# A state-space layer: decay rows broadcast over the partitions by DMA and masked by GpSimd, the exponential written to PSUM and multiplied from there

## The chip, the cores and the metric

The kernel runs on one core of a Trainium2 chip. The metric is the device time of one execution in microseconds. The kernel before has a median of 2572.7 us over three runs, between 2570.35 and 2581.11.

## What is computed

Two transformer-like layers on 1024 tokens (4 sequences of 256) of 512 features: attention and a sparse feed-forward part, then a state-space layer and a feed-forward part. The change is in the state-space layer alone. It has 128 heads of 64 channels in 8 groups; B and C (128 states) are shared by the 16 heads of a group. Cut to what matters here:

```python
dt = clip(softplus(dt + dt_bias), 0.001, 100)
cs = cumsum(dt * A, axis=time)                 # per head; A = -1 .. -128
Lmat = where(l >= s, exp(cs[l] - cs[s]), 0)    # per head and sequence, 256 x 256
y[l] = sum_s (C[l] . B[s]) * Lmat[l, s] * dt[s] * x[s]
y = y + D * x
out = rmsnorm_per_group(y * silu(gate)) * norm_w @ out_proj.T
```

(The reference scans in chunks of 128; the kernel takes a whole sequence of 256 at once, which is the same sum.)

## The kernel before

**Tiling.** A group g is worked in 8 units j. A unit is 2 heads = 128 channels on the partitions, with 1024 tokens along the columns, in two halves of 512. For each unit TensorE projects four halves (`in_half`: X_0, X_1, G_0, G_1, that is x and the gate), each 12 matmuls of 128x512, since weights and input are split in a high and a low part and multiplied three times. ScalarE takes the last convolution tap from PSUM (`tap`), VectorE the three others (`conv_tap`), ScalarE a tanh, VectorE makes SiLU of it (`silu`).

**The scan.** It goes sequence by sequence, b = 0 to 3. For one (j, b) and one head, s lies on the partitions and l along the columns. Since l >= s, of the 256 x 256 matrix only 384 columns are worked: s in the first block against l of both blocks (256 columns), s in the second block against l of the second (128 columns). The parts:

- `rows` (PE): a matmul with a one-hot column broadcasts the head's row of -cs over the 128 partitions, into PSUM bank 5. The row comes from `comb`, where it lies as three bfloat16 parts that add up to it.
- `clamp` (ScalarE): Relu(row + cs[s]), with cs[s] as bias per partition, from PSUM into the buffer `decay`. For l < s the clamp gives 0.
- `exps` (ScalarE): Exp(-...) over both heads at once, 768 columns, in place.
- `decay` (VectorE): times the scores `b_scores`, into `decayed`. The scores are C.B times a mask of 0.25 and 0, made once a group (`scores`).
- `scan` (PE): `decayed` against `xdt` (x times dt, transposed by `turn` on PE and scaled by `times_dt` on VectorE).
- `skip` (VectorE) adds D*x, `gate` (GpSimd) multiplies by SiLU of the gate, `square` (ScalarE) and `add_square` (GpSimd) gather the squares for the norm. `sq` is one buffer of 512 columns.

**Order.** There is no scheduler: each engine runs its own written sequence (`steps`), and semaphores join them. In step j TensorE projects unit j+1 while it scans unit j. `decay` and `decayed` have two buffers each, by b % 2. GpSimd also makes the low parts of the weights (`weights_lo`), for which SP's next load (`load_in`) waits, three buffers in a ring. Between two groups stand `unit0` (the last step's convolution work) and `project` (norm and output projection). Groups 0 to 6 are a loop, group 7 is written out behind it. ScalarE's order in step j, for j >= 1:

```
exps(j,1)  tap X0  weights_hi  square(j-1,0)  exps(j,2)  tanh X0  tap X1  exps(j,3)
square(j-1,1)  tanh X1  tanh G0  weights_hi  exps(j+1,0)  tanh G1
```

VectorE's:

```
decay(j,0)  conv X0 tap 1  decay(j,1)  skip(j-1,1)  conv X0 taps 2, 3  decay(j,2)  conv X1 tap 1  silu X0
conv X1 taps 2, 3  skip(j,0)  silu X1  silu G0  decay(j,3)  silu G1  times_dt twice
```

Lines: L964 clamp, L970 exponential, L1242 `decay`, L1461 `rows`, L1473 and L1474 `scan`, L1451 to L1453 `in_half`, L1206 convolution, L1226 and L1232 SiLU, L938 `tap`, L954 tanh, L1131 `weights_lo`, L1144 `gate`, L1152 `add_square`.

## Time and profile before

| | |
|---|---|
| median of three runs | 2572.7 us (2570.35 to 2581.11) |
| span of the profiled execution | 2581.9 us; no other time of it is at hand |
| PE / VectorE / ScalarE / GpSimd busy | 2390.2 / 1761.2 / 1368.2 / 802.0 us |
| `rows`, TensorE (L1461) | 512 matmuls |
| clamp and exponential, ScalarE (L964, L970) | 344.2 and 216.7 us |
| `decay`, VectorE (L1242) | 256, 397.9 us, 1554 ns on average |

Busy is the time in which an engine works on at least one instruction; sums over lines can be longer, since neighbours overlap. A chain of waits over the whole program says little here, because the engines are nearly balanced in this layer: what counts is the order within one unit, and so the timeline of one unit is shown below.

### The profile page before, as it was taken

What the parts mean: (1) busy time and instruction counts of PE and PEld (TensorE: products, weight loads), DVE (VectorE), ACT (ScalarE), POOL (GpSimd) and SP (SyncE); (2) the same over time, 40 slices, a digit from 0 to 9 for tenths busy, and PEclk for the clock granted to TensorE, in tenths of its full rate; (3) what the DMA queues carried; (4) which work ended last, traced back from release to release, by engine and by line L of the source; (5) the groups of instructions that cost most, each with busy time, mean ns of one, the idle gap of its engine ahead of it and who ended that gap; (6) DMA issues with size and microseconds to landing.
All of it is one profiled execution on the core that took longest, in us unless ns stands there. A gap on an engine that the chain in (4) does not pass through costs nothing. (4 is left out here: it accounts for less than half of the span.)

```text
span 2581.9 us, 39470 instructions
## 1 busy us (share of the span) xinstructions
PE 2390.2 (93%) x11656; PEld 1672.8 (65%) x11656; DVE 1761.2 (68%) x3109; ACT 1368.2 (53%) x3069; POOL 802.0 (31%) x645
## 2 busy tenths in 40 slices
PE   7989989899799989999989999998999999987998
PEld 4445454454567767767677676776766767756877
DVE  4656566464689579759848957966984985975345
ACT  5325152250488468548638737845854874873230
POOL 3214041130134325414414423432441441441220
PEclk8998989899899999999999999999999999998999
DMA  5000000000211011011011010101101101101100
GB/s 196 1 1 0 0 1 0 1 1 0 94 30 34 23 46 34 19 50 34 27 43 34 27 47 27 33 14 55 34 23 46 34 27 45 34 1 74 49 17 33
DMA packets 36024, 82.95 MB, mean 32 GB/s; under 512 B 3664, under 2 KB 3792, under 8 KB 35168
## 3 DMA queue, kind: packets, MB, share of 16 engines
q1 hardware_dynamic: 35808, 80.38, 9.5%
q8 instruction: 98, 1.61, 0.3%
q14 instruction: 118, 0.97, 0.1%
HBM read 77.48 MB, written 2.88 MB: 31 GB/s over the span
## 5 line engine op out<-in xcount | busy, mean ns | idle before, releaser
L1451 PE MATMUL b_ps<-xh_keep,wh 128*128 128x512 f32 x1152 | 495.3, 430 | 23.1 <-issue 20.1
L1453 PE MATMUL b_ps<-xh_keep,wl 128*128 128x512 f32 x1152 | 468.0, 406 | 0.0
L1452 PE MATMUL b_ps<-xl_keep,wh 128*128 128x512 f32 x1152 | 467.7, 406 | 0.0
L1242 DVE TENSOR_TENSOR decayed<-decay,b_scores 128x768 f32<-128x768 f32 x256 | 397.9, 1554 | 25.7 <-ACT decay L970 24.8
L1131 POOL TENSOR_TENSOR wl<-wraw,wh 128x512 fp32r<-128x512 f32 x144 | 190.6, 1324 | 606.9 <-ACT wh L919 606.9
L1206 DVE SCALAR_TENSOR_TENSOR xs<-b_ps,par,xs 128x510 f32<-128x510 f32 (+2 forms) x384 | 284.7, 742 | 119.9 <-ACT xs L938 107.0
L964 ACT ACTIVATE decay<-b_ps,cs 128x256 f32<-128x256 f32 (+1 forms) x1024 | 344.2, 423 | 7.9 <-PE b_ps L1461 7.7
L1451 PEld LDWEIGHTS b_ps<-xh_keep,wh 128*128 128x128 f32 x1152 | 224.6, 195 | 103.6 <-issue 59.8
L1453 PEld LDWEIGHTS b_ps<-xh_keep,wl 128*128 128x128 f32 x1152 | 224.2, 195 | 54.3
L1452 PEld LDWEIGHTS b_ps<-xl_keep,wh 128*128 128x128 f32 x1152 | 225.6, 196 | 43.1
L1332 DVE SCALAR_TENSOR_TENSOR yl<-yg,par,yh 128x512 fp32r<-128x512 f32 x128 | 96.4, 758 | 201.9 <-ACT yh L985 200.8
L970 ACT ACTIVATE decay<-decay 128x768 f32<-128x768 f32 x256 | 216.7, 846 | 8.1
L1552 PE MATMUL b_ps<-oh,yh 128*128 128x512 f32 x512 | 202.0, 395 | 12.8 <-DVE yl L1332 12.2
L1144 POOL TENSOR_TENSOR yg<-yt,yg 128x512 f32<-128x512 f32 x112 | 180.8, 1615 | 100.6 <-DVE yt L1261 100.5
L985 ACT ACTIVATE yh<-yg,par 128x512 fp32r<-128x512 f32 x128 | 91.7, 722 | 211.4 <-PE b_ps L1554 211.4
L1553 PE MATMUL b_ps<-oh,yl 128*128 128x512 f32 x512 | 200.2, 391 | 0.0
L1554 PE MATMUL b_ps<-ol,yh 128*128 128x512 f32 x512 | 200.0, 391 | 0.0
L1473 PE MATMUL b_ps<-decayed,xdt 128*64 128x256 f32 x1024 | 174.4, 416 | 21.3 <-DVE decayed L1242 21.2
L1152 POOL TENSOR_TENSOR ssq<-ssq,sq 128x512 f32<-128x512 f32 x112 | 144.9, 1293 | 152.8 <-ACT sq L978 152.8
L938 ACT ACTIVATE xs<-b_ps,par 128x512 f32<-128x512 f32 x128 | 98.4, 769 | 137.8 <-PE b_ps L1453 137.8
L296 POOL TENSOR_SCALAR pr<-pr,su 128x256 f32<-128x256 f32 x128 | 118.1, 923 | 108.6 <-DVE su L435 108.6
L1136 POOL TENSOR_TENSOR ol<-oraw,oh 128x512 fp32r<-128x512 f32 x64 | 85.6, 1337 | 210.6 <-ACT oh L926 210.6
(225 smaller groups left out, 4258.2 us busy)
## 6 DMA issues: line engine op xcount, KB each, us to landing
wraw<-win_dram SPq DMA_DIRECT2D x144, 256.0 KB, 2.6
oraw<-wout_dram SPq DMA_DIRECT2D x8, 2048.0 KB, 9.7
w<-w_dram SPq DMA_DIRECT2D x2, 3584.0 KB, 23.7
fraw<-wgu_dram SPq DMA_DIRECT2D x11, 512.0 KB, 3.3
draw<-wd_dram SPq DMA_DIRECT2D x1, 2816.0 KB, 11.2
out_dram<-x_keep SPq DMA_DIRECT2D x8, 256.0 KB, 2.0
wqkv<-wqkv_dram SPq DMA_DIRECT2D x1, 1536.0 KB, 9.1
x_keep<-x_dram SPq DMA_DIRECT2D x1, 1536.0 KB, 30.7
```

Of the source, the lines that this page charges most:

```text
L964: last = nc.scalar.activation(dst, src, ACT.Relu, bias=bias)
L970: nc.scalar.activation(ex[:, b % 2, :, :], ex[:, b % 2, :, :], ACT.Exp, scale=-1.0).then_inc(*exp_done.inc())
L1131: nc.gpsimd.tensor_tensor(wl[:, n % RING, :], wraw[:, n % RING, :], wh[:, n % RING, :].bitcast(F32), ALU.subtract).then_inc(w_lo.sem, 1)
L1144: nc.gpsimd.tensor_tensor(yg[:, j, cols], yt[:, h, :], sg, ALU.mult).then_inc(*gated.inc())
L1206: ins = nc.vector.scalar_tensor_tensor(y[:, :, back:], z[:, :, 0:SEQ - back], param(g, sub, TAPS - 1 - back), y[:, :, back:], ALU.mult, AL ...
L1242: nc.vector.tensor_tensor(sd[:, b % 2, :, :], ex[:, b % 2, :, :], sm[:, b, :].unsqueeze(1).to_broadcast([P, 2, 3 * P]), ALU.mult)\
L1451: nc.tensor.matmul(out, w_h, x_h, start=(k == 0), stop=False)
L1452: nc.tensor.matmul(out, w_h, x_l, start=False, stop=False)
L1453: last = nc.tensor.matmul(out, w_l, x_h, start=False, stop=(k == KT - 1))
L1552: nc.tensor.matmul(ps[t][:], y_h, oh[:, j % 2, :], start=(j == 0), stop=False)
L1553: nc.tensor.matmul(ps[t][:], y_l, oh[:, j % 2, :], start=False, stop=False)
L1554: last = nc.tensor.matmul(ps[t][:], y_h, ol[:, j % 2, :], start=False, stop=(j == UNITS - 1))
```

## The change

The broadcast over partitions goes from TensorE to the DMA queues: the rows of -cs (float32, stored once in DRAM) are read per unit with a partition broadcast into `rows`, two buffers of two heads, four sequences and three blocks of 128 columns, of which the DMA fills the first two. GpSimd (`mask_rows`) adds a constant (0 or a large negative number, `later`) to the two diagonal blocks, one of them into the third place. ScalarE then takes Exp(row - cs[s]) straight from there, without a clamp, and writes it to PSUM, bank 4 for head 0 and bank 5 for head 1. VectorE multiplies from PSUM, one product a head, each with its own semaphore count. The three-way split of the sums in the prologue goes. Banks of other jobs move to make room, and the scores are copied by ScalarE (times 0.25) where VectorE masked them before.

```diff
-        ("pick", (p[:, None] % 32 == np.arange(16)[None, :])),
+        ("later", np.where(p[None, :] >= p[:, None], 0.0, -BIG)),
...
-        ex = sb("decay", [P, 2, 2, 3 * P])
+        rows = sb("rows", [P, 2, 2, BATCH, 3, P])
         sd = sb("decayed", [P, 2, 2, 3 * P])
...
+        EXP_BANK = 4
...
-                for b in range(BATCH):
-                    out.append((f"R{j}_{b}", 5))
-                    out += nxt[b:b + 1]
+                out += nxt
                 if j < UNITS - 1:
-                    out += [(f"Y{j}_0", 6), (f"T{j + 1}_0", 4), (f"T{j + 1}_1", 6), (f"Y{j}_1", 7)]
+                    out += [(f"Y{j}_0", 6), (f"T{j + 1}_0", 6), (f"T{j + 1}_1", 1), (f"Y{j}_1", 7)]
...
-        head_jobs = [(f"CB{b}", 4 + b) for b in range(BATCH)] + [("T0_0", 4), ("T0_1", 6)]
+        head_jobs = [("CB0", 6), ("CB1", 7), ("CB2", 2), ("CB3", 3), ("T0_0", 6), ("T0_1", 7)]
...
+        def decay_of(g, j, b, h):
+
+            at = rows[:, j % 2, h, b]
+            c0, c1 = (ncs[:, ds(g * HPG + ((b * TPB + t) * NH + 2 * j + h), 1)] for t in range(TPB))
+            e = ps[EXP_BANK + h]
+            yield e[:, 0:2 * P].rearrange("p (k c) -> p k c", c=P), at[:, 0:2, :], c0
+            yield e[:, 2 * P:3 * P], at[:, 2, :], c1
...
+            def load_rows(g, j):
+
+                src = ssm["cs_dram"][ds(g * HPG + 2 * j, 2), :].rearrange("h (b c) -> h b c", b=BATCH)
+                for h in range(2):
+                    sp.dma_start(rows[:, j % 2, h, :, 0:2, :].rearrange("p b k c -> p b (k c)"),
+                                 src[h].partition_broadcast(P)).then_inc(rows_loaded[j % 2], 16)
...
+                sp.wait_ge(*exp_done.made(ph, heads[0], back=1))
+                load_rows(i, 1)
                 for n in range(AHEAD, AHEAD + SUBS):
                     load_in(i, n)
                     if n == AHEAD:
                         load_out(i)
-                sp.wait_ge(*bk.filled(ph, f"R{UNITS - 1}_{BATCH - 1}"))
-                load_comb(i + 1)
-            for n in range(AHEAD, SUBS):
-                load_in(LOOPS, n)
-                if n == AHEAD:
-                    load_out(LOOPS)
+                    j = (n - AHEAD) // 2 - 1
+                    if n % 2 == 0 and 0 <= j < UNITS - 1:
+                        sp.wait_ge(*exp_done.made(ph, (j, BATCH - 1, 1)))
+                        load_rows(i, j + 2)
...
-            def clamp(ph, g, j, b):
-
-                name = f"R{j}_{b}"
-                if b >= 2 or j:
-
-                    act.wait_ge(*decayed.made(ph, f"{j}_{b - 2}" if b >= 2 else f"{j - 1}_{b + 2}"))
-                waited(bk.filled(ph, name))
-                for src, dst, bias in blocks(ph, g, j, b):
-                    last = nc.scalar.activation(dst, src, ACT.Relu, bias=bias)
-                last.then_inc(*bk.free(ph, name))
-
             def exps(ph, g, j, b):
-                clamp(ph, g, j, b)
-                act.wait_ge(*bk.drained(ph, f"R{j}_{b}"))
-                nc.scalar.activation(ex[:, b % 2, :, :], ex[:, b % 2, :, :], ACT.Exp, scale=-1.0).then_inc(*exp_done.inc())
+
+                act.wait_ge(*rows_masked.made(g, j))
+                for h in range(2):
+                    if j or b:
+                        waited(decayed.made(ph, (j, b - 1, h) if b else (j - 1, BATCH - 1, h)))
+                    else:
+                        act.sem_inc(act_passed)
+                    for dst, src, bias in decay_of(g, j, b, h):
+                        last = nc.scalar.activation(dst, src, ACT.Exp, bias=bias)
+                    last.then_inc(*exp_done.inc())
+
+            def scores(ph):
+
+                for b in range(BATCH):
+                    name = f"CB{b}"
+                    act.wait_ge(*bk.filled(ph, name))
+                    nc.scalar.activation(sm[:, b, :], ps[bk.bank(ph, name)][:, 0:3 * P], ACT.Copy, scale=0.25)\
+                        .then_inc(*bk.free(ph, name))
...
+            def mask_rows(g, j):
+
+                pool.wait_ge(rows_loaded[j % 2], g * (32 * UNITS // 2) + 32 * (j // 2 + 1))
+                later = cst("later").unsqueeze(1).to_broadcast([P, 2 * BATCH, P])
+                at = rows[:, j % 2].rearrange("p h b k c -> p (h b) k c")
+                nc.gpsimd.tensor_tensor(at[:, :, 2, :], at[:, :, 1, :], later, ALU.add)
+                nc.gpsimd.tensor_tensor(at[:, :, 0, :], at[:, :, 0, :], later, ALU.add).then_inc(rows_masked.sem, 1)
...
+                    if j < UNITS - 1:
+                        mask_rows(g, j + 1)
+                    if j:
                         add_square(ph, j - 1)
...
                 steps(ph, i, False)
+                mask_rows(i, UNITS)
                 add_square(ph, UNITS - 1)
...
-                dve.wait_ge(*exp_done.made(ph, f"{j}_{b}"))
-                nc.vector.tensor_tensor(sd[:, b % 2, :, :], ex[:, b % 2, :, :],
-                                        sm[:, b, :].unsqueeze(1).to_broadcast([P, 2, 3 * P]), ALU.mult)\
-                    .then_inc(*decayed.inc())
+                for h in range(2):
+                    dve.wait_ge(*exp_done.made(ph, (j, b, h)))
+                    nc.vector.tensor_tensor(sd[:, b % 2, h, :], ps[EXP_BANK + h][:, 0:3 * P], sm[:, b, :], ALU.mult)\
+                        .then_inc(*decayed.inc())
...
-            def rows(ph, j, b):
-
-                name = f"R{j}_{b}"
-                pe.wait_ge(*bk.freed(ph, name))
-                for h in range(2):
-                    last = nc.tensor.matmul(ps[bk.bank(ph, name)][:, h * SEQ:(h + 1) * SEQ], sel[:, 2 * j + h:2 * j + h + 1].to_broadcast([32 * SPLITS, P]),
-                                            comb[:, b * SEQ:(b + 1) * SEQ], start=True, stop=True)
-                last.then_inc(*bk.full(ph, name))
...
-                    if j:
-                        rows(ph, j, 1)
                     for b in range(BATCH):
-                        if names and (j or b != 1):
+                        if names:
                             in_half(ph, g, 4 + 2 * j + b // 2, names[b])
-                        if b == 0:
-                            if j:
-                                scan(ph, j - 1, BATCH - 1)
-                            else:
-                                rows(ph, 0, 0)
-                                in_half(ph, g, 4, names[1])
-                                rows(ph, 0, 1)
-                        if b + 2 < BATCH:
-                            rows(ph, j, b + 2)
-                        elif b + 2 == BATCH and not final:
-                            rows(ph, j + 1, 0)
                         if b == 0 and j:
+                            scan(ph, j - 1, BATCH - 1)
                             pe.wait_ge(*bk.drained(ph, f"T{j}_1"))
                         if b + 1 < BATCH:
                             scan(ph, j, b)
```

The other hunks follow from these: `scores` on ScalarE, `ncs` for `cs` with the sign turned, the prologue without `sum_part` and `remainder`, and the same SP loop written out for the last group.

What stands in the queues, shown at three places. On ScalarE at the end of a step, `exps(j+1, 0)` and the tanh of G1 behind it. Before:

```order
L964 ISA [waits b_decayed,b_full5]
L964 ACTIVATE decay<-b_ps5,cs 128x256
L964 ISA
L964 ACTIVATE decay<-b_ps5,cs 128x128
L964 ISA
L964 ACTIVATE decay<-b_ps5,cs 128x256
L964 ISA
L964 ACTIVATE decay<-b_ps5,cs 128x128
L969 REGISTER_ALU
L970 ACTIVATE decay<-decay 128x768 [waits b_free5]
L947 REGISTER_ALU
L954 ACTIVATE tx<-b_ps3 128x512 [waits b_full3,silued]
```

And with the change:

```order
L926 REGISTER_ALU [waits rows_masked]
L977 ISA [waits b_decayed]
L977 ACTIVATE b_ps4<-rows,ncs 128x256
L977 ISA
L977 ACTIVATE b_ps4<-rows,ncs 128x128
L926 REGISTER_ALU
L977 ISA [waits b_decayed]
L977 ACTIVATE b_ps5<-rows,ncs 128x256
L977 ISA
L977 ACTIVATE b_ps5<-rows,ncs 128x128
L959 REGISTER_ALU
L966 ACTIVATE tx<-b_ps3 128x512 [waits b_full3,silued]
```

Four clamps and one exponential in place become four exponentials; the one wait at the head (the product two b earlier, and the filled bank) becomes a wait for each head on `b_decayed`, which is now the product of the b just before.

On GpSimd in the middle of a step, from `gate` (L1144, now L1159) to the first `add_square` (L1152, now L1167). Before:

```order
L1144 TENSOR_TENSOR yg<-yt,yg 128x512 [waits b_free7]
L1149 REGISTER_ALU
L1151 ISA [waits squared]
L1152 TENSOR_TENSOR ssq<-ssq,sq 128x512 [waits sq_added]
L1149 REGISTER_ALU
L1151 REGISTER_ALU [waits squared]
L1152 TENSOR_TENSOR ssq<-ssq,sq 128x512 [waits sq_added]
```

And with the change:

```order
L1159 TENSOR_TENSOR yg<-yt,yg 128x512 [waits b_free7]
L1143 REGISTER_ALU
L1146 TENSOR_TENSOR rows<-rows,consts 128x8x128 [waits rows_loaded0]
L1147 TENSOR_TENSOR rows<-rows,consts 128x8x128
L1164 REGISTER_ALU
L1166 ISA [waits squared]
L1167 TENSOR_TENSOR ssq<-ssq,sq 128x512 [waits sq_added]
L1164 REGISTER_ALU
L1166 REGISTER_ALU [waits squared]
L1167 TENSOR_TENSOR ssq<-ssq,sq 128x512 [waits sq_added]
```

The two additions on the rows of the next unit stand between `gate` and `add_square`.

On TensorE, the end of a projected half, and the scan behind it. Before:

```order
L1453 MATMUL b_ps2<-xh_keep,wl 128x512
L1459 REGISTER_ALU
L1461 MATMUL b_ps5<-comb,sel 128x256 [waits b_free5]
L1461 MATMUL b_ps5<-comb,sel 128x256
L1468 REGISTER_ALU
L1469 REGISTER_ALU [waits b_free7]
L1473 MATMUL b_ps7<-decayed,xdt 64x256 [waits b_decayed]
```

And with the change:

```order
L1459 MATMUL b_ps2<-xh_keep,wl 128x512
L1465 REGISTER_ALU
L1466 REGISTER_ALU [waits b_free7]
L1470 MATMUL b_ps7<-decayed,xdt 64x256 [waits b_decayed]
L1471 MATMUL b_ps7<-decayed,xdt 64x128
```

The two broadcast matmuls with their wait on bank 5 are gone, and the scan follows the projection. In step 0 of a group the second projection stood before scan(0, 0), and now stands behind it.

## Rows read from the trace of the kernel before

**Rows 1.** The page's list of DMA queues: packets, MB, share of 16 engines.

```profile
q1 hardware_dynamic: 35808, 80.38, 9.5%
```

**Rows 2.** Windows, one unit: length, busy us by engine, clock granted, DMA share, GB/s.

```profile
974.93:991.86 16.93, 16.93 (x100) 12.20 (x98) 15.71 (x19) 14.12 (x31) 8.38 (x6) 1.00 0.13 32
```

**Rows 3.** Timeline of PE: start, length, instruction, in an inner unit.

```profile
945.61 0.40 PE L1461 MATMUL b_ps<-comb,sel 96*128 96x256 bf16 x2
945.94 0.66 PE L1473 MATMUL b_ps<-decayed,xdt 128*64 128x256 f32 x4
...
946.74 0.50 PE L1451 MATMUL b_ps<-xh_keep,wh 128*128 128x512 f32 x1
```

**Rows 4.** Timeline of VectorE (DVE), one unit.

```profile
970.23 1.94 DVE L1242 TENSOR_TENSOR decayed<-decay,b_scores 128x768 f32<-128x768 f32 x1
972.64 0.69 DVE L1232 SCALAR_TENSOR_TENSOR yg<-tx,b_ps 128x512 f32<-128x512 f32 x1 [0.46 <-ACT tx L954]
973.24 1.28 DVE L1251 TENSOR_TENSOR xdt<-b_ps,dth 128x512 f32<-128x512 f32 x2
974.44 0.95 DVE L1242 TENSOR_TENSOR decayed<-decay,b_scores 128x768 f32<-128x768 f32 x1
975.86 0.75 DVE L1206 SCALAR_TENSOR_TENSOR xs<-b_ps,par,xs 128x510 f32<-128x510 f32 x1 [0.47 <-ACT xs L938]
976.53 1.89 DVE L1242 TENSOR_TENSOR decayed<-decay,b_scores 128x768 f32<-128x768 f32 x1
978.34 0.73 DVE L1261 SCALAR_TENSOR_TENSOR yt<-xs,par,b_ps 128x512 f32<-128x512 f32 x1
979.00 1.62 DVE L1206 SCALAR_TENSOR_TENSOR xs<-b_ps,par,xs 128x508 f32<-128x508 f32 x2
980.54 1.95 DVE L1242 TENSOR_TENSOR decayed<-decay,b_scores 128x768 f32<-128x768 f32 x1
...
983.07 0.68 DVE L1226 SCALAR_TENSOR_TENSOR xs<-tx,xs 128x512 f32<-128x512 f32 x1
983.67 1.52 DVE L1206 SCALAR_TENSOR_TENSOR xs<-b_ps,par,xs 128x508 f32<-128x508 f32 x2
...
987.15 1.95 DVE L1242 TENSOR_TENSOR decayed<-decay,b_scores 128x768 f32<-128x768 f32 x1
```

**Rows 5.** Timeline of ScalarE (ACT), the same unit.

```profile
968.36 0.63 ACT L954 ACTIVATE tx<-xs 128x512 f32<-128x512 f32 x1 [0.69 <-DVE xs L1206]
968.90 0.58 ACT L954 ACTIVATE tx<-b_ps 128x512 f32<-128x512 f32 x1
...
969.90 1.34 ACT L964 ACTIVATE decay<-b_ps,cs 128x256 f32<-128x256 f32 x4
...
972.02 0.58 ACT L954 ACTIVATE tx<-b_ps 128x512 f32<-128x512 f32 x1
...
974.93 0.78 ACT L938 ACTIVATE xs<-b_ps,par 128x512 f32<-128x512 f32 x1 [0.21 <-PE b_ps L1453]
```

**Rows 6.** Timeline of GpSimd (POOL), the same unit.

```profile
976.30 1.30 POOL L1131 TENSOR_TENSOR wl<-wraw,wh 128x512 fp32r<-128x512 f32 x1 [2.98 <-ACT wh L919]
...
980.38 1.29 POOL L1152 TENSOR_TENSOR ssq<-ssq,sq 128x512 f32<-128x512 f32 x1
```

**Rows 7.** Groups of instructions by line, shapes apart: count, busy us, mean ns.

```profile
L1268 DVE TENSOR_TENSOR b_scores<-b_ps,scan_mask 128x384 f32<-128x384 f32 x32 | 15.5, 546 | 0.0
...
L1792 POOL TENSOR_TENSOR fl<-fraw,fh 128x1024 fp32r<-128x1024 f32 x11 | 26.3, 2392 | 98.3 <-ACT fh L1747 98.3
```

**Rows 8.** Window and timeline of PE at the start of a group's unit 0.

```profile
914.00:937.00 23.00, 19.95 (x85) 13.87 (x86) 11.79 (x14) 14.83 (x32) 4.41 (x3) 0.78 0.06 19
...
923.48 0.39 PE L1461 MATMUL b_ps<-comb,sel 96*128 96x256 bf16 x2 [1.61 <-ACT decay L964]
```

**Rows 9.** Timeline between two groups: ScalarE's last square, TensorE's first output matmul.

```profile
1067.05 0.63 ACT L978 ACTIVATE sq<-yg 128x512 f32<-128x512 f32 x1 [2.14 <-POOL ssq L1152]
...
1073.80 0.49 PE L1552 MATMUL b_ps<-oh,yh 128*128 128x512 f32 x1 [1.12 <-DVE yl L1332]
```

More of the change, by code:

```diff
@@ L818, in ssm_layer, with mid @@
         silued = tally("silued", lambda c: c[0] if c[1] else None)
-        def mid(name, names):
-            return Tally(sem(name), [], names, names)
-        units, pairs = range(UNITS), [(j, b) for j in range(UNITS) for b in range(BATCH)]
-        exp_done = mid("b_exp_done", [f"{j}_{b}" for j, b in pairs])
-        decayed = mid("b_decayed", [f"{j}_{b}" for j, b in pairs])
+        def mid(name, names, credit=0):
+            return Tally(sem(name), [], names, names, credit=credit)
+        units, heads = range(UNITS), [(j, b, h) for j in range(UNITS) for b in range(BATCH) for h in range(2)]
+        exp_done = mid("b_exp_done", heads, credit=1)
+        decayed = mid("b_decayed", heads)
+        rows_loaded = [sem(f"rows_loaded{k}") for k in range(2)]
+        rows_masked = Signal(sem("rows_masked"), UNITS)
         scanned = mid("scanned", [(j, b) for j in units for b in (0, 2)])
@@ L884, in _ @@
                 load_in(0, n)
-            sp.wait_ge(parts, SPLITS)
-            for s in range(SPLITS):
-                sp.dma_start(ssm["cs_dram"][s], part[s]).then_inc(kept, 16)
-            sp.wait_ge(kept, 16 * SPLITS)
-            sp.wait_ge(zeroed, 1)
-            load_comb(0)
+            ph = Phase("pro", 0, 0)
+            for k in range(2):
+                sp.wait_ge(*bk.drained(ph, f"cT{k}"))
+            sp.dma_start(ssm["cs_dram"], csT).then_inc(kept, 16)
+            sp.wait_ge(kept, 16)
+            load_rows(0, 0)
             load_in(0, AHEAD - 1)
@@ L1109, in _ @@
             unit0(ph, 0)
+            scores(ph)
             with act.Fori(0, LOOPS) as i:
@@ L1115, in _ @@
                 project(ph, i, 1)
+                for h in range(2):
+                    act.wait_ge(*bk.drained(ph, f"o{EXP_BANK + h}"))
+                scores(ph)
             ph = Phase("epi", 0, LOOPS)
@@ L1262, in skip, with scored @@
                                                ps[bk.bank(ph, name)][:], ALU.mult, ALU.add).then_inc(*bk.free(ph, name))
-            def scores(ph):
+            def scored(ph):
                 for b in range(BATCH):
-                    name = f"CB{b}"
-                    dve.wait_ge(*bk.filled(ph, name))
-                    nc.vector.tensor_tensor(sm[:, b, :], ps[bk.bank(ph, name)][:, 0:3 * P], ssm["mask"][:], ALU.mult)\
-                        .then_inc(*bk.free(ph, name))
+                    dve.wait_ge(*bk.drained(ph, f"CB{b}"))
             def unit0(ph, g, last=None):
@@ L1402, in step_sizes @@
                 nc.vector.tensor_scalar(ssm["dth"][:], v, 0.5, None, ALU.mult)
-            def remainder(s):
-                dve.wait_ge(parts, s + 1)
-                nc.vector.tensor_tensor(csT, csT, part[s], ALU.subtract).then_inc(left, 1)
             ph = Phase("pro", 0, 0)
@@ L1422, in _ @@
             unit0(ph, 0)
-            scores(ph)
             times_dt(ph, 0, 0, 0)
             times_dt(ph, 0, 0, 1)
+            scored(ph)
             with dve.Fori(0, LOOPS) as i:
@@ L1599, in _ @@
                     pe.wait_ge(*bk.freed(ph, name))
-                last = nc.tensor.transpose(ps[bk.bank(ph, name)][:, (t % 4) * P:(t % 4 + 1) * P], ssm["cs"][:, t, :], cst("ident"))
+                last = nc.tensor.transpose(ps[bk.bank(ph, name)][:, (t % 4) * P:(t % 4 + 1) * P], ssm["ncs"][:, t, :], cst("ident"))
                 if t % 4 == 3:
```

73 lines of the change are left out of this document (27 added, 46 removed).

## The prediction

> **What bounds the kernel now.** The layer is eight groups of eight units, and 48 of these 64 are alike, so I read one of them. From the page I keep only the transfer queue's load [rows 1]. The unit by windows [rows 2]: 16.93 us, TensorE busy for all of it, VectorE for 15.71, ScalarE for 14.12, GpSimd for 8.38. TensorE is the bound, and VectorE is only 1.2 us behind it. The timelines of the four engines in a unit [rows 3 to 6] give the order and the lengths that the rest is worked from. I call "pitch" the time from one start to the next; it is shorter than a duration, since an engine overlaps the tail of one instruction with the next.
>
> **What goes.** TensorE loses the four pairs of row-broadcast matmuls of a unit. A pair takes 945.94 - 945.61 = 0.33 us [rows 3], so its work falls to 16.93 - 1.32 = 15.6 us. ScalarE loses the 768-wide exponential in place: from the first clamp (969.90) to the next tanh (972.02) a (j, b) pair holds it for 2.12 us [rows 5], four times a unit, and will hold it for about 1.4. VectorE loses the 768-wide product of two SBUF operands: 0.95 us alone, but 1.89 to 1.95 in three of four cases [rows 4]. The reason is in rows 6: the product that starts at 976.53 ends at 978.42, which is 0.82 after GpSimd's instruction (976.30 + 1.30 = 977.60). It had to wait until GpSimd was through. Its replacement, two 384-wide products with one operand in PSUM, has a twin in the old scores product [rows 7]: 0.546 us, four in 1.94, so a pitch of 0.46. A (j, b) pair then costs 0.93 instead of up to 1.95, and VectorE's work falls by 6.7 - 3.7 = 3 us to about 12.7.
> The Trainium skill (SBUF — State Buffer, "Who interferes with whom") states that a VectorE instruction with at most one SBUF input does not contend with GpSimd, and one with two does, against a GpSimd instruction that reads SBUF. By it the new products run free, and the SiLU of x (tx and xs both in SBUF) does not. The trace shows the second half, in the 1.89 against 0.95.
>
> **What comes.** Three things, and none is on TensorE.
> (1) The exponentials of one head: 256 and 128 wide, from SBUF to PSUM. Not in the trace. Four PSUM-to-SBUF clamps of the same widths take 1.34 us [rows 5], so a pair is at least 0.60; at most it is 0.89, were nothing overlapped and each 0.1 longer than a clamp. Reading SBUF costs a tanh 0.63 against 0.58 [rows 5], so I take 0.62 + 0.1 = 0.70 as pitch, 0.78 to the end.
> The Trainium skill (ScalarE: Activation LUTs, "Step-by-step: what each stage is for") says that ScalarE writes PSUM faster than SBUF, without a figure. That speaks for the low end; with 0.60 the unit below would be 0.4 us shorter. No row here shows such a write.
> (2) The order. There is one PSUM bank per head, so exps(j, b) of a head cannot start before decay(j, b-1) of that head is done, where the old buffer gave a whole b of room. exps(j+1, 0) stands before the last tanh of a unit, exps(j, 1) before the next tap. So tanh and tap now wait behind VectorE.
> (3) The mask: two GpSimd additions of 1024 columns a unit. The nearest row is a 1024-wide subtraction, 2.39 us [rows 7]; a 512-wide addition takes 1.29 [rows 6]. I take 2.36 each, between 2.3 and 3.2 (strided operands may cost more). It stands between gate and add_square. Queued behind it is add_square(j-1, 0), for which ScalarE's square(j-1, 1) waits (sq is a single buffer), and behind that square stands tanh X1.
>
> **An inner unit after the change**, from the start of decay(j-1, 3) = 0. A wait ended by another engine costs 0.04 (tanh 972.02 + 0.58 to 972.64 [rows 4, 5]), 0.15 where the instruction takes a register operand (tap 974.93 + 0.78 to 975.86).
> VectorE's products end at 0.55 and 1.01. ScalarE: exps(j, 0) at 0.70 and 1.40, tanh G1 at 2.10 to 2.68. VectorE: SiLU G1 2.72, times_dt 3.32, decay(j, 0) at 4.52, head 0 done 5.07. ScalarE: exps(j, 1) 5.22 and 5.92, tap X0 6.62 to 7.40. VectorE: first conv tap 7.55, decay(j, 1) 8.22, skip 9.15 to 9.89, taps two and three 9.81, decay(j, 2) 11.35. ScalarE: tanh X0 11.47, tap X1 12.01 to 12.79. VectorE: conv tap of X1 12.94, SiLU X0 wants to start at 13.60.
> GpSimd: gate 9.92 to 11.20 (as long as an addition), mask 11.16 to 13.52 and 13.48 to 15.84. SiLU X0 finds the second half of the mask running and ends 0.55 after it, at 16.4; taps two and three run to 17.9; tanh X1 to 18.6. GpSimd: add_square(j-1, 0) 15.8 to 17.1; ScalarE's square to 17.8; add_square(j-1, 1) 17.8 to 19.1. SiLU X1, wanted at 18.7, is held again, to 19.7. SiLU G0, then decay(j, 3) at 20.2.
> So a unit takes 20.2 instead of 16.93: +3.3. TensorE, with 15.6 of work, then idles for 4.6 in each.
>
> **The sum**, for a group in the loop. Units 2 to 6: 5 x 3.3 = 16.5. Unit 1 has the mask but no add_square: +2.9. Unit 7 has no mask in it: +0.5 (longer from decay to tap). Unit 0: TensorE loses two waits for the clamps, 1.61 [rows 8] and another about as long, but scan(0, 0) now stands before the second projection and waits about 3 for exponential and product; part of the half-speed stretch there goes: -1.5, between -4 and 0. Between groups: the mask of the next unit 0 (4.7) stands before the last two add_squares. ScalarE's square waited 2.14 for these already [rows 9], the tap of X0_1 is behind it, and after it come conv, SiLU and the yl that TensorE waited 1.12 for at 1073.80: +4.7 in full. Stalls are followed by stretches at 1.2 GHz: in 914 to 937, where unit 0 has its stalls, the granted clock was 0.78 [rows 8]. I put +1.3 for it. A group: 16.5 + 2.9 + 0.5 - 1.5 + 6 = 24.4, seven times 171. The last group has no next one: 16.5 + 2.9 - 1.5, and its unit 7, a chain of exponentials, gets 1.6 shorter: 16. The prologue loses the three-way split of the decay sums from ScalarE and VectorE: -2. Sum +185 us.
> The profiled execution has a span of 2581.9, and the three runs a median of 2572.7, so it is 9 us above it; I add the sum to the median: 2758, rounded 2760.
>
> **What is hidden.** The row transfers: 2 x 512 KB a unit, in packets of 1 KB, 1024 of them on 16 engines. The queue's packets took 0.095 x 16 x 2581.9 / 35808 = 0.11 us each, at 2.2 KB a piece [rows 1], so 64 a engine take 3 to 7 us. SP issues them at about 0.5 of the unit (behind load_in, which waits for the last weight remainder), the mask wants them at 11.2. If that cover went, each us of lateness would add one to the unit. The scores, now copied by ScalarE, fall where it has nothing else to do.
>
> **Rivals.**
> A, the hand-over alone: the mask fits into GpSimd's idle half and holds nobody. For it: GpSimd is idle 8.5 us a unit [rows 2]. Against it: add_square behind it in the queue. Without the mask's two holds the walk gives decay(j, 3) at 17.7: +0.8 a unit, 6 units x 0.8 + 0.5 - 1.5 + 2 between groups, eight times: +46, so 2617. 10%.
> B, the other side, faster: TensorE stays the bound. For it: it is the bound today, and all three busy engines lose work. It needs the loop over ScalarE and VectorE to close within 15.6, thus 2.1 less than even without the mask, with eight hand-overs shorter than I take them. Then 8 x 1.32 and the 3 us of unit 0 go per group, eight times: -109, 2464. It decides from a unit under 16.9. 8%.
> C, TensorE falls to half clock for good: it idles 4.6 in 20.2, and after stalls of 1.6 the clock is at 1.2 GHz for a while today [rows 8]. 15.6 of work fit into 20.2 as long as less than 45% of the time is at half speed; at 70% a unit takes 24: +3.8 x 48 more, about 2940. 8%.
> D, the rows come late (packets twice as slow as the bound above, landing at 15): +4 x 48, 2950. 6%.
> The forecast itself has 68%; its own range, from the mask's 2.3 to 3.2 us and the exponentials' 0.60 to 0.89 (four of them in the loop of a unit), is 2715 to 2870 (both high ends at once would give 2885).
>
> **How the numbers follow.** Faster than now by over 0.5% (about what can be told from no change): B alone, 8%. Within 0.5%: 2%, a thin part of A. Slower: 90%. The range 2650 to 2870 leaves out B, A at its centre and the upper parts of C and D, 20% or a little more in all.
>
> **What would show it.** Right: inner units of about 20 us; TensorE waiting for products and for the SiLU (before the transposes) for over 4 us a unit; SiLU rows of xs at 1.5 to 3 us instead of 0.69; ScalarE's square waiting for GpSimd's ssq; the new products at 0.55 throughout; each mask half near 2.4. Wrong: units under 17 with TensorE without idle time (B); units of 17.7 and short squares' waits (A); a granted clock under 0.8 in the units (C); masks waiting for the DMA of rows (D). A mask half much longer than 3.2 us would move all of it upward.

## The result, and the profile after

The changed kernel takes 2762.6 us (median of 4 runs, 2756.5 to 2769.4) against 2574.4 us for the kernel before on the same chip (4 runs, 2570.4 to 2581.1): ratio 1.073, 95% interval 1.071 to 1.075. The forecast was 2760. The profiled execution took 2761.8 us, with a span of 2760.0 and a mean granted clock of 0.929 (before: 0.953).

First the whole-program groups of the page after (line, engine, output<-inputs, count | busy us, mean ns | idle us just before them, and who ended it):

```profile
L977 ACT ACTIVATE b_ps<-rows,ncs 128x256 f32<-128x256 f32 (+1 forms) x1024 | 372.2, 410 | 258.6 <-DVE decayed L1263 228.4
...
L1263 DVE TENSOR_TENSOR decayed<-b_ps,b_scores 128x384 f32<-128x384 f32 x512 | 260.8, 548 | 5.8 <-ACT b_ps L977 4.5
...
L1478 PE MATMUL b_ps<-consts,xs 128*128 128x128 f32 x512 | 88.2, 328 | 128.5 <-DVE xs L1246 128.3
...
L1246 DVE SCALAR_TENSOR_TENSOR xs<-tx,xs 128x512 f32<-128x512 f32 x128 | 125.8, 984 | 106.9 <-ACT tx L966 104.9
L1147 POOL TENSOR_TENSOR rows<-rows,consts 128x1024 f32<-128x1024 f32 x64 | 177.7, 2776 | 0.0
```

The products got about as cheap as they were meant to: 548 ns, two for a pair (j, b), where [rows 4] had up to 1.95 us. And yet ScalarE waits 228 us for VectorE, TensorE 128 us for the SiLU ahead of its transposes (`turn`), and VectorE 105 us for a tanh. Three engines wait for each other in a circle: each wait is ended by an instruction that itself stands behind the next wait. Two neighbouring inner units, to be held against [rows 2] (length, busy us by engine, granted clock, DMA share, GB/s):

```profile
985.84:1006.77 20.93, 16.18 (x90) 11.55 (x89) 13.83 (x23) 11.43 (x26) 13.07 (x9) 1.00 0.25 76
1006.77:1027.70 20.93, 17.57 (x90) 12.70 (x89) 13.83 (x23) 11.43 (x26) 13.06 (x9) 0.92 0.25 76
```

A unit takes 20.93 us instead of 16.93. VectorE and ScalarE are busy for 1.9 and 2.7 us less, GpSimd for 4.7 more. TensorE is busy for 16.18 us at a granted clock of 1.00 and idle for the other 4.75; in the second unit it is busy for 17.57 us because it ran slower in part of it (0.92). The length is the same.

The circle is read from the timelines of the second unit. GpSimd (start, length, instruction, [idle before <-who ended it]):

```profile
1016.80 1.29 POOL L1159 TENSOR_TENSOR yg<-yt,yg 128x512 f32<-128x512 f32 x1 [0.67 <-DVE yt L1281]
1018.04 2.41 POOL L1146 TENSOR_TENSOR rows<-rows,consts 128x1024 f32<-128x1024 f32 x1
1020.39 2.93 POOL L1147 TENSOR_TENSOR rows<-rows,consts 128x1024 f32<-128x1024 f32 x1
1023.28 1.26 POOL L1167 TENSOR_TENSOR ssq<-ssq,sq 128x512 f32<-128x512 f32 x1
```

ScalarE:

```profile
1012.08 1.46 ACT L977 ACTIVATE b_ps<-rows,ncs 128x256 f32<-128x256 f32 x4 [2.59 <-DVE decayed L1263]
1013.48 0.76 ACT L950 ACTIVATE xs<-b_ps,par 128x512 f32<-128x512 f32 x1
...
1019.57 1.45 ACT L977 ACTIVATE b_ps<-rows,ncs 128x256 f32<-128x256 f32 x4
1024.58 0.63 ACT L994 ACTIVATE sq<-yg 128x512 f32<-128x512 f32 x1 [3.56 <-POOL ssq L1167]
1025.12 0.61 ACT L966 ACTIVATE tx<-xs 128x512 f32<-128x512 f32 x1
```

VectorE:

```profile
1009.53 0.69 DVE L1252 SCALAR_TENSOR_TENSOR yg<-tx,b_ps 128x512 f32<-128x512 f32 x1 [1.74 <-ACT tx L966]
...
1011.33 1.01 DVE L1263 TENSOR_TENSOR decayed<-b_ps,b_scores 128x384 f32<-128x384 f32 x2
1014.39 0.75 DVE L1226 SCALAR_TENSOR_TENSOR xs<-b_ps,par,xs 128x510 f32<-128x510 f32 x1 [2.05 <-ACT xs L950]
1015.05 1.01 DVE L1263 TENSOR_TENSOR decayed<-b_ps,b_scores 128x384 f32<-128x384 f32 x2
1015.98 0.74 DVE L1281 SCALAR_TENSOR_TENSOR yt<-xs,par,b_ps 128x512 f32<-128x512 f32 x1
...
1020.37 0.68 DVE L1246 SCALAR_TENSOR_TENSOR xs<-tx,xs 128x512 f32<-128x512 f32 x1
...
1025.76 1.42 DVE L1246 SCALAR_TENSOR_TENSOR xs<-tx,xs 128x512 f32<-128x512 f32 x1 [2.62 <-ACT tx L966]
...
1027.70 1.01 DVE L1263 TENSOR_TENSOR decayed<-b_ps,b_scores 128x384 f32<-128x384 f32 x2
```

Follow it once round: decay(j, 0) at 1011.33 frees the PSUM bank; exps(j, 1) 1012.08; the tap behind them 1013.48; conv tap 1014.39, decay(j, 1), skip 1015.98; GpSimd's gate 1016.80; the two mask halves 1018.04 and 1020.39; add_square 1023.28; ScalarE's square, which waited 3.56 us for it, 1024.58; tanh X1; SiLU X1 1025.76; decay(j, 3) 1027.70; and from there exponentials, tanh G1 and SiLU G1 to the next decay(·, 0). In this chain each step starts within 0.2 us of the end of the one before it, and TensorE is hardly in it: the unit is 20.93 us long whether TensorE needs 16.18 or 17.57 us for its work.

Between two groups, GpSimd, ScalarE and TensorE, to be held against [rows 9]:

```profile
1098.11 2.41 POOL L1146 TENSOR_TENSOR rows<-rows,consts 128x1024 f32<-128x1024 f32 x1
1100.48 2.40 POOL L1147 TENSOR_TENSOR rows<-rows,consts 128x1024 f32<-128x1024 f32 x1
```

```profile
1104.17 0.63 ACT L994 ACTIVATE sq<-yg 128x512 f32<-128x512 f32 x1 [5.77 <-POOL ssq L1167]
```

```profile
1110.88 0.79 PE L1536 MATMUL b_ps<-oh,yh 128*128 128x512 f32 x1 [2.29 <-DVE yl L1350]
```

Where the time went, from the starts of the products in the VectorE timelines (group 1; for the three lines between groups the mean over the six gaps between groups 0 to 6; the output matmuls are counted by the first of each three, L1552 before and L1536 after), in us:

| stretch | before | after | difference | forecast |
|---|---|---|---|---|
| unit 1: decay(0, 3) to decay(1, 3) | 18.74 | 17.71 | -1.0 | +2.9 |
| unit 2 | 17.35 | 20.87 | +3.5 | +3.3 |
| units 3 to 6, each | 16.93 | 20.94 | +4.0 | +3.3 |
| unit 7 | 19.00 | 19.76 | +0.8 | +0.5 |
| seven units together | 122.8 | 142.1 | +19.3 | +19.9 |
| last decay to first output matmul | 16.9 | 21.5 | +4.7 | +4.7 |
| output matmuls, first to last | 43.8 | 46.1 | +2.3 | +1.3 |
| last output matmul to decay(0, 3) of the next group | 28.1 | 25.4 | -2.7 | -1.5 |
| group | | | +23.6 | +24.4 |

Seven groups of 23.9 (mean of all distances from first decay to first decay) are 167 us. The rest of the 178 us between the two spans is the last group, +20 (forecast 16), and a prologue shorter by 9.5 in this pair of executions. That last number can't be put to the change (the forecast's -2 for it isn't to be resolved here): the three variants of the kernel before that were profiled below, with its prologue unchanged, reach the first decay at 700.3, 702.0 and 707.2, the changed kernel at 701.0, the kernel before at 710.5. The medians differ by 188 us and not by 178, since the profiled execution of the kernel before has a span 7.5 us above its median.

### The profile page after: what moved, and what is told of

Its sections match the earlier page's. It is cut to its first block and busy times, and to the rows that moved or that the text cites. A ratio compares the mean times of both kernels' runs of the same rounds, so it can differ in the third digit from the quotient of the medians.

```text
span 2760.0 us, 39344 instructions
## 1 busy us (share of the span) xinstructions
PE 2390.3 (87%) x11144; PEld 1686.8 (61%) x11144; DVE 1640.4 (59%) x3327; ACT 1206.5 (44%) x2842; POOL 1092.3 (40%) x773
## 5 line engine op out<-in xcount | busy, mean ns | idle before, releaser
L1457 PE MATMUL b_ps<-xh_keep,wh 128*128 128x512 f32 x1152 | 510.4, 443 | 14.6 <-issue 13.9
L977 ACT ACTIVATE b_ps<-rows,ncs 128x256 f32<-128x256 f32 (+1 forms) x1024 | 372.2, 410 | 258.6 <-DVE decayed L1263 228.4
L1458 PE MATMUL b_ps<-xl_keep,wh 128*128 128x512 f32 x1152 | 478.2, 415 | 0.0
L1457 PEld LDWEIGHTS b_ps<-xh_keep,wh 128*128 128x128 f32 x1152 | 234.2, 203 | 97.3 <-issue 52.0
L1263 DVE TENSOR_TENSOR decayed<-b_ps,b_scores 128x384 f32<-128x384 f32 x512 | 260.8, 548 | 5.8 <-ACT b_ps L977 4.5
L1458 PEld LDWEIGHTS b_ps<-xl_keep,wh 128*128 128x128 f32 x1152 | 233.2, 202 | 44.1
L1536 PE MATMUL b_ps<-oh,yh 128*128 128x512 f32 x512 | 209.4, 409 | 20.4 <-DVE yl L1350 19.8
L1478 PE MATMUL b_ps<-consts,xs 128*128 128x128 f32 x512 | 88.2, 328 | 128.5 <-DVE xs L1246 128.3
L1246 DVE SCALAR_TENSOR_TENSOR xs<-tx,xs 128x512 f32<-128x512 f32 x128 | 125.8, 984 | 106.9 <-ACT tx L966 104.9
L1147 POOL TENSOR_TENSOR rows<-rows,consts 128x1024 f32<-128x1024 f32 x64 | 177.7, 2776 | 0.0
L1159 POOL TENSOR_TENSOR yg<-yt,yg 128x512 f32<-128x512 f32 x112 | 147.5, 1317 | 63.1 <-DVE yt L1281 63.1
L1167 POOL TENSOR_TENSOR ssq<-ssq,sq 128x512 f32<-128x512 f32 x112 | 142.9, 1276 | 57.5 <-ACT sq L994 57.5
```

What stands on the lines that cost most here:

```text
L977: last = nc.scalar.activation(dst, src, ACT.Exp, bias=bias)
L1147: nc.gpsimd.tensor_tensor(at[:, :, 0, :], at[:, :, 0, :], later, ALU.add).then_inc(rows_masked.sem, 1)
L1263: nc.vector.tensor_tensor(sd[:, b % 2, h, :], ps[EXP_BANK + h][:, 0:3 * P], sm[:, b, :], ALU.mult)\
L1457: nc.tensor.matmul(out, w_h, x_h, start=(k == 0), stop=False)
L1458: nc.tensor.matmul(out, w_h, x_l, start=False, stop=False)
L1536: nc.tensor.matmul(ps[t][:], y_h, oh[:, j % 2, :], start=(j == 0), stop=False)
```

## Experiments

Nine kernels were run, in three batches on three chips, each batch with runs of the kernel before beside it (e1 to e4: 2578.2 us; e5, e6: 2573.8; e7 to e9: 2572.9). All times are medians, the ratio is to the kernel before on the same chip; where two experiments of different batches are subtracted, some 5 us of the difference can be the chip's.

### The mask out of the circle (e1_mask_early)

```
 GpSimd, steps():
-    if more: weights_lo(g, 6 + 2 * j)
-    if j: gate(ph, j - 1, (1,))
-    if j < UNITS - 1: mask_rows(g, j + 1)
-    if j: add_square(ph, j - 1)
+    if j < UNITS - 1 or not last: mask_rows(g, j + 1)
+    if more: weights_lo(g, 6 + 2 * j)
+    if j:
+        gate(ph, j - 1, (1,))
+        add_square(ph, j - 1)
 between groups:
-    mask_rows(i, UNITS)
 SyncE: the rows' DMA
-    if n % 2 == 0 and 0 <= j < UNITS - 1:
+    if n % 2 == 1 and 0 <= j < UNITS - 1:
```

> Same work as the changed kernel; only the order on GpSimd differs: in each step the two mask additions of the next unit come first (ahead of the gate of the unit before), those for the next group's first unit in step 7 instead of between the groups, and the rows' DMA is issued one weight load earlier. Theory (place of the mask): the changed kernel's unit of 20.94 us is a ring that goes through skip, gate, both mask halves, add_square, ScalarE's square, tanh X1, SiLU X1, decay; with the mask out of the ring units 1 to 6 fall to the 17.7 us that the changed kernel's first step shows, where no add_square stands behind the mask, unit 7 stays near 19.8, and between the groups 4.7 us go. That is 5 x 3.2 + 4.7 = 21 us per group less, 2594 us (2585 to 2610). Rival (GpSimd's load as such, two additions of 2.4 us at the port that it shares with VectorE, makes the unit longer wherever they stand): units stay near 20.9, 2730 to 2765 us. Rival (hand-over of the exponentials alone is the cost): the same as the rival before, no gain.

Measured: 2589.4 us (2581.2 to 2600.5, 10 runs), ratio 1.006 [1.004, 1.008], within my interval. Units 1 to 6 at 17.71, unit 7 at 19.77. One unit, then its mask, and a square that follows the exponentials at once:

```profile
972.13:989.85 17.72, 16.19 (x90) 11.57 (x89) 13.12 (x24) 11.47 (x26) 12.38 (x9) 1.00 0.29 91
```

```profile
974.54 2.38 POOL L1146 TENSOR_TENSOR rows<-rows,consts 128x1024 f32<-128x1024 f32 x1
976.88 2.36 POOL L1147 TENSOR_TENSOR rows<-rows,consts 128x1024 f32<-128x1024 f32 x1
```

```profile
984.95 1.45 ACT L977 ACTIVATE b_ps<-rows,ncs 128x256 f32<-128x256 f32 x4
986.33 0.62 ACT L994 ACTIVATE sq<-yg 128x512 f32<-128x512 f32 x1
```

The same two additions, at another place in one queue, cost 173 us less (the rows' transfers start one weight load earlier as well, but GpSimd had not waited for them in the changed kernel). So it is the place of the mask's 4.7 us of work that cost these 173 us, and not the work as such.

### Only the buffer between (e2_two_sq)

```
+def sq_of(j, h):      # a second square buffer, in sg0's free half
+    return sg0[:, 0:HALF] if h and j < UNITS - 1 else sq[:]
 square(): ScalarE
-    if j + h >= 2: act.wait_ge(*sq_added.made(ph, (j, 0) if h else (j - 1, 1)))
+    if j >= 2: act.wait_ge(*sq_added.made(ph, (j, 0) if j == UNITS - 1 and h else (j - 1, h)))
```

> The changed kernel with the mask where it is, and a second buffer for ScalarE's square of a unit's second half, so that it no longer waits until GpSimd has added the first half. Theory: the mask's place costs its time through this one buffer alone. Without the wait ScalarE's tanh X1 starts some 2.5 us earlier in the unit; SiLU X1 is then held only by the port. The unit falls from 20.9 to between 17.7 and 18.7 us, which over 5 or 6 units in 8 groups is 2640 to 2670 us. Rival (GpSimd's load, or the time VectorE is held at the port by the mask): no change, 2750 to 2765.

Measured: 2626.5 us (2622.9 to 2630.7), ratio 1.020 [1.017, 1.023], below my interval. Mask and queue are as in the changed kernel, and the second mask half still takes 2.92 us, but the square no longer waits for GpSimd, and follows the exponentials at once:

```profile
995.21 1.44 ACT L980 ACTIVATE b_ps<-rows,ncs 128x256 f32<-128x256 f32 x4
996.60 0.62 ACT L997 ACTIVATE sg<-yg 128x512 f32<-128x512 f32 x1
```

```profile
982.40:1000.11 17.71, 16.18 (x90) 11.56 (x89) 13.11 (x23) 11.47 (x26) 13.34 (x9) 1.00 0.28 90
```

The unit is 17.71, the same as with the mask moved: the 3.2 us a unit went through this one wait, and what VectorE and GpSimd cost each other by running at the same time ("the port" in the expectations) adds nothing behind it. What e1 has over e2, 37 us, lies between the groups, where the mask still stands: from the last decay to the first output matmul 21.5 us in e2 against 17.1 in e1, 31 us in seven gaps, and the output matmuls, 1.1 us longer, give another 8.

### Only ScalarE's order (e3_act_order)

```
 ScalarE, steps():
-    exps(ph, g, j, 1)
     act.wait_ge(*bk.drained(ph, f"Y{j - 1}_0"))
     tap(ph, gn, h[0])
+    exps(ph, g, j, 1)
 ...
+    tanh(ph, h[3])
     if j < UNITS - 1:
         exps(ph, g, j + 1, 0)
-    tanh(ph, h[3])
```

> The changed kernel with two changes of order on ScalarE alone: the tap of the first X half ahead of the unit's second pair of exponentials, and the tanh of the B/C half ahead of the next unit's first pair of exponentials. The mask stays in its place. Theory (a ring over three engines): four exponentials and what they wait for leave the ring, which shortens it by 3.7 us by the changed kernel's own rows, so the unit falls from 20.9 to about 17.3 us, 2585 us (2570 to 2640). Rival (the mask alone holds the unit, whatever ScalarE's order): the unit stays at 20.9, 2750 to 2765.

Measured: 2684.4 us (2682.8 to 2686.9), ratio 1.042 [1.039, 1.044]. The direction is right, the size isn't, and the time is outside my interval: units of 18.5 and 20.1 instead of 17.3.

```profile
992.09:1010.60 18.51, 15.98 (x89) 11.71 (x88) 14.33 (x23) 11.41 (x27) 12.98 (x9) 0.99 0.31 86
1010.60:1030.73 20.13, 17.60 (x91) 13.11 (x90) 14.35 (x23) 11.41 (x27) 12.96 (x9) 0.92 0.27 79
```

My walk had left TensorE out. With the exponentials gone from ScalarE's path, the next link is TensorE: SiLU X1 (1008.67 to 1010.09), then this row, then twelve projection matmuls, then the tap.

```profile
1010.14 1.93 PE L1478 MATMUL b_ps<-consts,xs 128*128 128x128 f32 x8 [2.53 <-DVE xs L1246]
```

```profile
1015.87 0.78 ACT L950 ACTIVATE xs<-b_ps,par 128x512 f32<-128x512 f32 x1 [3.06 <-issue]
```

From the end of the SiLU to the tap is 5.8 us here. The eight transposes took 1.93 us instead of the 1.09 that eight took in the changed kernel (at 1006.31, at full clock): TensorE had stood idle for 2.53 us, and its granted clock then went to 1.2 GHz (0.53 of full from 1010.1 to 1012.1). The two lengths of a unit differ by 1.62 us, and so do the busy times of TensorE in them (17.60 - 15.98): in this circle the clock is paid in full, since TensorE is a link of it. In the changed kernel, where it isn't, units 3 to 6 are 20.94 with such a stretch in them and without.

### The same load in the kernel before (e4_before_mask, e8_before_add_early)

```
+def add_rows(g, j, spare):    # two 1024-wide additions on GpSimd, their result unused
+    for k in range(2):
+        nc.gpsimd.tensor_tensor(spare[k]..., ssm["dth"][:], tri, ALU.add)
 e4, GpSimd, steps():                    e8:
     weights_lo(g, 6 + 2 * j)           +    if 0 < j < UNITS - 1: add_rows(...)
     if j: gate(ph, j - 1, (1,))             weights_lo(g, 6 + 2 * j)
+    if j < UNITS - 1: add_rows(...)         if j: gate(ph, j - 1, (1,))
     if j: add_square(ph, j - 1)        +    if j == 0: add_rows(...)
 both, between groups: + add_rows(...)       if j: add_square(ph, j - 1)
```

> The kernel before with one thing added: two GpSimd additions of the mask's size and operand types in the mask's place (behind the gate, ahead of the additions of squares; between the groups for unit 0). Their result is used by nothing; all else is as before, the 16 row matmuls of a unit and the exponentials in SBUF included. Theory (place of the mask): units 2 to 6 go from 16.93 to about 19.5 us and between the groups 4.7 us are added; 5 x 2.6 + 4.7 = 18 us per group, about 2700 us (2670 to 2740). Rival (hand-over of PSUM and exponentials is the cost, not GpSimd): 2575 to 2595 us.

> The kernel before with the same two unused GpSimd additions per unit as in the run that put them at the mask's place, but at the start of GpSimd's steps 1 to 6 (in step 0 and between the groups they stay where they were). It tells the place of GpSimd's work from its amount. The time with them at the mask's place was 2789 us, without them 2574. Theory (place): units 2 to 6 fall back most of the way, since add_square no longer stands behind them; what stays is the additions between the groups, 4.7 us in each, and the time that VectorE's SBUF instructions (a multiplication of the scores takes 0.95 us alone and 1.9 held) are held by 4.7 us of GpSimd more per unit: 2640 to 2690 us. Rival (amount: in this kernel, whose VectorE reads SBUF with both inputs, two more additions of 2.4 us cost the same wherever they stand): 2760 to 2800 us.

Measured: e4 2788.9 us (2786.2 to 2796.6), ratio 1.083 [1.080, 1.086], above my interval, which was worked out at full clock; e8 2661.5 us (2660.1 to 2663.3), ratio 1.034 [1.032, 1.036], within it. A unit of e4 at either clock, and its square:

```profile
1015.62:1035.35 19.73, 17.15 (x97) 12.10 (x96) 18.57 (x19) 14.24 (x32) 14.43 (x9) 0.99 0.08 28
1035.35:1056.59 21.24, 18.67 (x100) 13.43 (x99) 18.55 (x19) 14.23 (x32) 14.40 (x9) 0.93 0.09 25
```

```profile
1053.47 0.63 ACT L979 ACTIVATE sq<-yg 128x512 f32<-128x512 f32 x1 [3.50 <-POOL ssq L1161]
```

And a unit of e8:

```profile
1015.52:1033.18 17.66, 17.10 (x98) 12.21 (x97) 16.54 (x19) 14.14 (x32) 15.16 (x9) 1.00 0.12 31
```

Neither the row matmuls (eight a unit, not the 16 of the expectation) nor the exponentials were touched, and the kernel before loses 2788.9 - 2578.2 = 211 us: more than by the whole change. Place and amount come apart here: 2788.9 - 2661.5 = 127 us for the place in steps 1 to 6, and 2661.5 - 2572.9 = 89 us for the two additions at another place in the units (0.7 us in each of units 3 to 6) plus the 4.7 us between the groups. The old form of the product has a part in this: VectorE is busy for 16.54 us in a unit of e8 and 18.57 in one of e4, against 15.71 in [rows 2], because its instructions with both operands in SBUF wait for GpSimd. The products come to 451.5 us in e4 and 443.4 in e8, against 397.9; most of e4's rest is the SiLU of x, which has 95.2 in the kernel before and 125.8 in the changed one. Its rows in e4, then in e8:

```profile
L1240 DVE SCALAR_TENSOR_TENSOR xs<-tx,xs 128x512 f32<-128x512 f32 x128 | 207.5, 1621 | 13.8 <-ACT tx L955 12.6
```

```profile
L1242 DVE SCALAR_TENSOR_TENSOR xs<-tx,xs 128x512 f32<-128x512 f32 x128 | 120.8, 944 | 6.8 <-ACT tx L955 1.1
```

The changed kernel's products, with one operand in PSUM, stay at 0.55 us beside the mask.

### Mask early and the order (e5, e6)

e5 is e1 and e3 together. e6 adds, on TensorE, the projection ahead of the first product of unit 0, which the kernel before had between its first row matmuls:

```
 TensorE, steps():
-    if names:
+    if names and (j or b != 1):
         in_half(ph, g, 4 + 2 * j + b // 2, names[b])
+    if j == 0 and b == 0:
+        in_half(ph, g, 4, names[1])
```

> Mask early on GpSimd and the order on ScalarE (tap ahead of the second pair of exponentials, tanh of the B/C half ahead of the next first pair), together. Theory: with the mask out of the ring what holds the unit at 17.71 us is a shorter ring of ScalarE and VectorE (decay, exponentials behind it, tanh, SiLU of the B/C half, the X half's tap and convolution), since TensorE's own work in a unit is 15.6 us; the order takes four waits of exponentials out of it, so the unit falls to between 15.6 and 16.4 us and TensorE bounds. From 2589 us: 6 units x 8 groups x 1.3 to 2.1 us is 62 to 101 us less, 2488 to 2527 us, up to 15 us less if unit 7 falls too. Rival (TensorE or the port bounds at 17.7 whatever the order): 2585 to 2595 us.

> As the run before, and TensorE's second projection of unit 1's first half put ahead of the first product of unit 0. Theory: at the start of a group TensorE waits for the first mask, exponentials and decay; the projection fills that wait, 1.5 to 2.5 us per group, 12 to 20 us less than the run before. Rival: what releases the first decay of a group is late anyway and the projection only moves the wait: within 5 us of the run before.

Measured: e5 2500.4 us (2494.7 to 2502.6), ratio 0.971 [0.969, 0.973], within my interval; e6 2463.0 us (2461.1 to 2470.7), ratio 0.957 [0.955, 0.959]. A unit of e5, and of e6:

```profile
979.75:995.52 15.77, 15.77 (x90) 11.79 (x89) 13.21 (x23) 11.36 (x26) 12.30 (x9) 1.00 0.33 95
```

```profile
975.65:991.42 15.77, 15.77 (x90) 11.79 (x89) 13.21 (x24) 11.36 (x26) 12.33 (x9) 1.00 0.34 103
```

TensorE is full again, and a unit is 1.16 us shorter than in [rows 2]. So 17.71 was the second circle, through ScalarE's exponentials, which wait for the product before them with the tap and the tanh behind them, as the order of these undoes it. That the single PSUM bank per head is what makes them wait was not tried apart: no run gave them a second one. The step in e6 was worth 37 us, twice what I had put on it: it takes the wait out of unit 1 as well (17.01 to 15.16 us) and not only from the first product.

### The order alone in the kernel before (e7_before_order)

The edit of e3, in the kernel before.

> The kernel before with only ScalarE's order changed as in the reordered version (tap ahead of the unit's second exponentials, tanh of the B/C half ahead of the next first exponentials). Theory (TensorE bounds the units of the kernel before, 16.93 us with the row matmuls in them): the order can't shorten units 3 to 7, only the wait in unit 1 (18.74 us) and between groups, so 2550 to 2580 us, and the gain of the reordered version needs the row matmuls gone. Rival (the order alone brings that gain and the change itself brings nothing): 2460 to 2500 us.

Measured: 2732.2 us (2720.3 to 2737.1), ratio 1.061 [1.059, 1.064]. Both theories missed: the order that gains 89 us with the mask early (e1 to e5) costs 159 here.

```profile
987.68 0.39 PE L1461 MATMUL b_ps<-comb,sel 96*128 96x256 bf16 x2 [1.12 <-ACT decay L964]
...
993.25 0.39 PE L1461 MATMUL b_ps<-comb,sel 96*128 96x256 bf16 x2 [1.51 <-ACT decay L964]
```

```profile
983.80:1003.74 19.94, 17.31 (x99) 12.20 (x98) 14.27 (x19) 14.23 (x30) 9.35 (x7) 1.00 0.09 28
```

The row matmuls stand in TensorE's queue and wait for a bank that ScalarE's clamps set free. Put the clamps behind the tap, and they wait for the projection, which stands behind those row matmuls: a circle of TensorE and ScalarE, 19.94 us long, in which the two waits shown are TensorE's whole idle time (19.94 - 17.31). The full TensorE of [rows 2] rested on the old order. The change takes this dependence away, for its rows come by DMA, and only then is the better order of e5 free.

### The last wait in the reordered kernel (e9_best_decay7)

```
 VectorE, steps(), j == 7:
-    conv(ph, gn, h[2])
     decay(ph, j, 3)
+    conv(ph, gn, h[2])
```

> The reordered version with TensorE's projection filling unit 0, and one change on VectorE: in step 7 the product of the last decay with the scores comes ahead of the three taps of the next group's third half instead of behind them. There TensorE waits 2.43 us for this product and its clock is 1.2 GHz for 3.4 us afterwards (step 7 takes 17.85 us against 15.77). Theory: step 7 of seven groups falls by the 2.1 us, 15 us in all, 2445 to 2452 us. Rival: the taps that now stand behind it are waited for in their turn (TensorE's turn of the B/C halves and the next unit's start), nothing is won: 2458 to 2468 us.

Measured: 2477.2 us (2475.1 to 2482.8), ratio 0.963 [0.961, 0.965]: 14 us slower than e6. Step 7 does fall, from 17.85 to 15.24 us, but from decay(7, 3) to the first output matmul it is now 1832.85 - 1812.64 = 20.21 us, where e6 has 1830.32 - 1813.45 = 16.87. TensorE's waits of e9 there:

```profile
1829.92 0.63 PE L1525 MATMUL b_ps<-consts,ssq 128*128 128x128 f32 x4 [3.11 <-DVE xs L1224]
1832.85 0.79 PE L1536 MATMUL b_ps<-oh,yh 128*128 128x512 f32 x1 [2.29 <-DVE yl L1348]
```

In e6 the second of these was 1.13 us. So step 7's 2.6 us come back as 3.3 here. Another 2.0 us a group are in the output matmuls (46.8 us from first to last against 44.8, means over six groups), as TensorE's granted clock over 1832.85 to 1880 is 0.94, and 1.00 in e6 over 1830.32 to 1876; 0.9 us are won back up to the next decay(0, 3). That makes about 1.9 us a group, and over seven groups the 14 us. The rival was right that nothing is won, and underpriced; both intervals missed.

## Why the prediction was right, point by point

- **What goes.** Right for TensorE, which is full at 15.77 us (e5), where the forecast had 15.6. The products take 548 ns throughout, but a pair takes 1.01 us, not 0.93, and VectorE's 12.7 us a unit was 13.83 (13.21 in e5): the SiLU of x, held behind GpSimd once a unit, was left out of it.
- **Exponentials to PSUM.** Right. Four of them take 1.46 us after, against the clamps' 1.34 in [rows 5]; the forecast was 0.70 a pair and 0.78 to the end, thus 1.48.
- **The mask.** Each half 2.4 us alone, as forecast (2.36), and the chain gate, mask, add_square, square, tanh X1, SiLU X1, decay(j, 3) is the one that the trace shows. e1 and e2 show it from two sides, e4 in another kernel.
- **The inner unit**, 20.2 forecast, 20.94 measured. The mis-sized term is the order at the port. I had SiLU X0 find the second mask half running; it started 0.02 us ahead of it (1020.37 against 1020.39), at 13.60 us from the start of the unit as forecast, while the mask half came 0.14 later than forecast; so GpSimd waited and the half took 2.93 us. Counted from the start of the unit, add_square started at 16.5 instead of 15.8 us, and SiLU X1, held like the forecast said, ended at 20.4 instead of 19.7: the same 0.7 up to decay(j, 3).
- **Unit 1**, +2.9 forecast, -1.0 measured: the step that failed. I had seen that no add_square stands behind the mask there, and priced the holds at the port all the same. With no add_square nobody waits for the mask, and the unit is 17.71, the length that I gave for the hand-over alone (17.7). Also, I took 16.93 for its length before, and it was 18.74.
- **The sum**, 185 us forecast, 188 measured, is this close in part by luck: two errors, +3.1 us in units 2 to 6 together and -3.9 in unit 1, nearly cancel in each group, and seven groups at 167 instead of 171 are made up by the last one at 20 instead of 16.
- **Between groups**: +4.7 as forecast. The output matmuls, part of them at 1.2 GHz (mean granted clock 0.94 from 1110.88 to 1157.5), cost 2.3 instead of the 1.3 us put on the clock, unit 0's gain 2.7 instead of 1.5.
- **The signs.** TensorE's idle time is there, 4.75 us in a unit at full clock, 1.39 of it for a product and 3.36 for the SiLU. The SiLU of x was to take 1.5 to 3 us; one of the two in a unit takes 1.42 and the other 0.68. ScalarE's square waits for `ssq` as announced.
- **Rivals.** A's cause was real but second in line: its 17.7 us a unit is what e1 and e2 leave (e1, with the gaps between groups also mended, 2589; A's terms add up to 2619, not 2617). B failed here because the loop over ScalarE and VectorE didn't close within 15.6; e6 closes it at 15.77, and lands on 2463 where B had 2464; that the two agree so closely is chance, since e6 needed a moved mask and two changes of order. C: the granted clock was 0.92 in the unit at 1006.77 and 1.00 in the one before it, and both are 20.93. D: rows landed 5.4 us after issue (median), and GpSimd had no idle time ahead of either mask half.

## What to carry to other kernels

Before work is added to an engine that looks idle, read what stands behind the new place in its queue and who waits for that: here 4.7 us of GpSimd work a unit cost 173 us more at one place than at another. Single buffers between engines (the square, the PSUM bank of a head) turn idle time into a circle; a second buffer or another place in the queue won 136 and 173 us here, while e1, with all the cheaper instructions in it, was still no faster than the kernel before. And an order that is right for one set of dependences is wrong for another: the same swap cost 159 us before the change and won 78 after it (e3), 89 with the mask out of the way (e1 to e5), so a change that removes a dependence is to be judged with the order that it makes possible.
